# One PSUM bank for C, copied behind both exponentials of a unit, in the state space layer of a 12-layer decoder kernel

## The reference, cut to what matters

```python
dA = exp(delta[..., None] * A)                        # (b, t, 512 channels, 16 states)
dBu = delta[..., None] * Bm[:, :, None, :] * u[..., None]
def step(h, inp):
    dA_t, dBu_t, C_t = inp
    h = dA_t * h + dBu_t
    y = einsum('bdn,bn->bd', h, C_t)
    return (h, y)
...
delta = softplus(einsum('blr,dr->bld', dt, Wdt) + bdt)
```

## Time and profile before

| | |
|---|---|
| timed runs | 4219.53, 4219.45, 4218.51 us; median 4219.45 |
| span of the profiled execution | 4219.3 us (0.15 under the median; the profile gives no time of its own beside the span) |
| busy over the span | PE 89%, DVE 73%, ACT 54%, POOL 33% |
| scans L1255 | 512, 590.7 us |
| products L1260 | 176, 215.0 us |
| exponentials L1220 | 512, 345.7 us |
| copies of C L1233 | 176, 103.1 us |

### The profile page before, as it was taken

One profiled execution on the slowest core, in us unless ns is written; L12 is line 12 of the kernel. 1 busy time (PEld: TensorE's weight loads), 2 busy tenths in 40 slices (PEclk: granted clock), 3 DMA queues, 4 the chain that ended last, 5 costly groups with the idle time before them and its releaser, 6 DMA issues. The chain is left out here.

```text
span 4219.3 us, 57578 instructions
## 1 busy us (share of the span) xinstructions
PE 3754.1 (89%) x20106; PEld 2591.3 (61%) x20106; DVE 3071.9 (73%) x7148; ACT 2286.6 (54%) x5527; POOL 1378.4 (33%) x937
## 2 busy tenths in 40 slices
PE   5777878777999998999999999888899889889998
PEld 2323333223666667998788887555566558645777
DVE  6989899897666667666787886677577784554777
ACT  5676767754644442222455556757677652343446
POOL 3989899995000000000233223366321100010000
PEclk8989989898999999999999999889999999988999
DMA  3444434344000000000000001000000000100000
GB/s 117 142 132 146 148 125 156 130 152 146 1 1 1 1 1 33 21 31 1 14 1 1 1 1 42 2 14 1 12 2 2 19 23 1 42 1 20 1 1 21
DMA packets 83283, 180.17 MB, mean 43 GB/s; under 512 B 9035, under 2 KB 14259, under 8 KB 80307
## 3 DMA queue, kind: packets, MB, share of 16 engines
q1 hardware_dynamic: 82995, 176.49, 12.5%
HBM read 173.84 MB, written 2.62 MB: 42 GB/s over the span
## 5 line engine op out<-in xcount | busy, mean ns | idle before, releaser
L209 PE MATMUL PS<-db,cst 128*128 128x512 f32 x1024 | 537.2, 671 | 159.7 <-DVE db L1260 159.7
L1255 DVE TENSOR_TENSOR_SCAN db<-PS,db 128x512 f32<-128x512 f32 x512 | 590.7, 1204 | 36.7 <-ACT PS L1220 27.9
L209 PEld LDWEIGHTS PS<-db,cst 128*128 128x128 f32 x1024 | 205.2, 211 | 466.9 <-DVE db L1260 244.6
L216 PE MATMUL PS<-cst,p 128*128 128x128 f32 (+1 forms) x2880 | 393.3, 282 | 48.1 <-DVE pt L3295 16.7
L216 PEld LDWEIGHTS PS<-cst,p 128*128 128x128 f32 (+1 forms) x2880 | 332.9, 147 | 106.7 <-issue 35.9
L209 PE MATMUL PS<-xnT,W 128*128 128x256 f32 (+2 forms) x1072 | 330.7, 455 | 19.4 <-ACT pt L2826 7.9
L1201 POOL TENSOR_TENSOR db<-W,b 128x1024 f32<-128x1024 f32 x128 | 312.5, 2470 | 1.9 <-PE PS L209 1.8
L1201 POOL TENSOR_TENSOR db<-du,b 128x1024 f32<-128x1024 f32 x128 | 307.9, 2432 | 6.6 <-PE PS L209 5.8
L209 PEld LDWEIGHTS PS<-xnT,W 128*128 128x128 f32 (+1 forms) x1072 | 210.2, 200 | 137.9 <-issue 89.0
L2035 POOL TENSOR_TENSOR rb<-rb,tb 128x512 f32<-128x512 f32 x32 | 42.9, 1342 | 758.2 <-DVE tb L2030 758.2
L1693 ACT ACTIVATE p<-PS,sm 128x333 f32<-128x333 f32 x320 | 168.7, 538 | 164.8 <-DVE sm L1686 161.9
(11 more groups left out here) (469 smaller groups left out, 8512.2 us busy)
## 6 DMA issues: line engine op xcount, KB each, us to landing
b<-bc_rows SPq DMA_DIRECT2D x256, 256.0 KB, 3.4
c<-bc_rows SPq DMA_DIRECT2D x256, 256.0 KB, 3.5
W<-in_we SPq DMA_DIRECT2D x9, 1024.0 KB, 4.8
W<-in_w SPq DMA_DIRECT2D x1, 4224.0 KB, 12.3
W<-in_w SPq DMA_DIRECT2D x1, 4122.5 KB, 14.0
W<-in_w SPq DMA_DIRECT2D x1, 4100.0 KB, 12.3
W<-in_w SPq DMA_DIRECT2D x1, 2313.0 KB, 8.3
X<-in_x SPq DMA_DIRECT2D x4, 512.0 KB, 14.5
```

Source lines behind the costliest of these rows:

```text
L209: ins = T.matmul(out, l, r, start=first and i == 0, stop=last and i == len(pairs) - 1)
L216: ins = T.transpose(bank[0:m, c:c + r], s, ident[0:r, 0:r])
L1255: V.tensor_tensor_scan(db[:, f, r], self.ring.PS[:, self.BANKS[x % 3], r], db[:, f, r], 0.0, ALU.mult, ALU.add).then_inc(self.sc.sem, 1)
```

## The change

CBANKS becomes (4,): C always goes to bank 4, and bank 3 stays in the ring, which so has four banks in this layer, two for y and two that go round. The copy of C moves on ACT from between the two exponentials of its unit to behind both. With one bank it waits until the product of the vector unit before it is done, h(n), where before it waited for the one before that, h(n - 1).

```diff
-    CBANKS = (3, 4)
+    CBANKS = (4,)
...
             C.activation(bank[:, :, lo:hi], split(self.delta[d], 4)[:, 2 * p + f, :].rearrange(
                 "p (b s) -> p b s", b=2)[:, :, lo:hi], ACT.Exp,
                 scale=self.As[d][:, 2 * p + f, s:s + 1]).then_inc(self.aa.sem, 1)
-            if f == 0 and not self.on_pool(i):
-                self.act_c(e, i)
+        if not self.on_pool(i):
+            self.act_c(e, i)

     def cbank(self, i):
-        return self.ring.PS[:, self.CBANKS[(i - self.pools(i)) % 2], :]
+        return self.ring.PS[:, self.CBANKS[0], :]

     def act_c(self, e, i):

         e.wait_ge(*self.cd_of(i))
-        e.wait_ge(*self.h(i - self.pools(i) - 1))
+        e.wait_ge(*self.h(i - self.pools(i)))
         e.eng.activation(self.cbank(i), self.c_[i % 4], ACT.Copy).then_inc(self.ca.sem, 1)
```

## The result

The changed kernel takes 4232.3 us (median of 20 runs, 4212.17 to 4234.45); the kernel before, run beside it, 4219.57 us (20 runs). The ratio is 1.0022, 95% interval [1.0012, 1.0031]: about 9 us slower by the ratio, 5 to 13 by its interval, where 8.6 was forecast. The medians lie 12.7 us apart, since the times of the changed kernel fall into two groups (4 of the 20 at 4212 to 4215, 16 at 4229 to 4234) and the median takes no account of the small one. The profiled execution has a span of 4229.7 us.

The account below looks back on a forecast made before the run. DVE, busy 888.8 of the layer's 961 us, was taken to set the pace. Waits of 14.5 us less 5.6 for the ring's bank gave 8.9, taken as 8.6: about 4228 us (+0.2%), own range 4223 to 4233.

Parts of the forecast that it names:

- Gate SiLU: Four piles on ACT behind a second unit: each DVE wait becomes 2.95 us, 7.3 us lost in all.
- ABS of odd k: Delta chains of k = 3, 5, 7: fourth evacuation and ABS start 1.64 us later, 4.9 us lost in all.
- waits 1.6 us longer in sum: Sign of being right: DVE's waits for ACT in the k = 3, 5, 7 chains grow by 1.6 us in sum.
- Square root: The next layer's square root, unit 12 mod 16, starts 2.31 us later with SILU's pile behind it; 2.3 us lost.
- Ring bank: Delta chains of k = 1, 2, 4, 6: a second bank going round lets delta matmuls come earlier; 5.6 us gained.
- The start: Start of the layer, where PE waited for banks too: may give back some tenths of a us.
- Part 3: Second exponential comes 0.52 us earlier where ACT is late; DVE waited for the first, so nothing is gained.
- Wrong if the y waits move by more than 2 us: Sign of being wrong: DVE's waits for PE ahead of y move over 2 us in either direction.
- the ring's bank reaches nothing: Rival, chance 0.17: PE's low clock makes the delta matmul late, not the bank; only the 14.5 us remain, 4234.
- ACT's being held costs nothing: Rival, chance 0.10: long piles on ACT start as before, only the 5.6 us gain counts, 4214.
- the second exponential is waited for: Rival, chance 0.05: DVE waited for the second exponential, so 25 waits shrink by 0.52, 13.0 us; 4215.
- The copy in DVE's path: Rival, chance 0.05: copy falls into DVE's path in the steady run, 0.2 us for each of 96 units; 4247.

Follow-up runs that it names:

- held at the gates: Kernel before, with the copy behind both exponentials and the later wait only at the four units ahead of a gate SiLU; 4221.3 us, ratio 1.0020.
- the shortened pile: Kernel before, C's second bank lent to the ring at times, copy behind both exponentials, each gate's last evacuation one step earlier; 4215.8 us, ratio 0.9999.
- first pair of traces: First profiles of the kernel before and of the changed kernel; medians 4219.57 and 4232.3 us, ratio 1.0022.
- all piles moved: Changed kernel with gate SiLU one step later, delta chains of k = 3, 5, 7 and the first square root one step earlier; 4231.3 us, ratio 1.0038.
- second pair of traces: Kernel before and changed kernel, both unchanged, profiled a second time; 4218.3 us (ratio 1.0008) and 4232.6 us (ratio 1.0037).
- the kernel without it: Changed kernel with bank 3 left idle, so three banks in the ring as before; 4242.9 us, ratio 1.0058.
- held copies: Kernel before, copy moved and waiting later at chosen units only: without long piles (1.0000), at gate SiLUs (1.0020), at ABS and square root (1.0030).
- the order alone: Kernel before with only the copy moved behind both exponentials, two banks for C and the old wait; 4221.8 us, ratio 1.0014.

## Why the prediction was right

- **What bounds the kernel.** Right: DVE's path carried every term, and DVE waited for no copy.
- **Gate SiLU, 7.3 us.** Measured 7.4, all four waits 2.96 for a forecast of 2.95, alone again in the kernel held at the gates. The rule of the room behind a unit also gave the 0.5 of the shortened pile, but with 4.0 us of room for two banks and a copy behind both exponentials, worked out later; the 4.4 of the prediction would give 0.1.
- **ABS of odd k, 4.9 us.** DVE's L1144 starts 1.64 us later, the number forecast. But the 1.64 does not stay as it is: 1.1 of it is won back right behind (at k = 3 waits of 0.41 and 0.79 us become 0 and 0.22), and 1.7 is lost anew, since L1144 and L1157 themselves get longer beside POOL (3.13 for 2.02, 2.50 for 1.92). So 2.2 us a chain remain, 6.6 in all, and that the term is no further off is luck. The sign "waits 1.6 us longer in sum" did not come: they are 0.5 longer, and the rest stands in the length of DVE's own instructions.
- **Square root, 2.3 us.** 2.4.
- **Ring bank, k = 2, 4, 6 and k = 1, 5.6 us.** 5.9 by the first pair of traces, 7.5 by the second, in which the kernel before had the longer waits at k = 2 and 4. The Trainium skill, Perfetto Trace Analysis, Optimizing Tensor Performance, has groups rotate through different PSUM banks; the trace agrees, and more than I took from it. The bank also makes these chains deaf to PE's clock: 17 of the 18 waits at k = 2, 4, 6 in the six profiles with two banks to go round and the copy behind both exponentials are 1.76 or 1.77 at granted clocks from 0.50 to 1.00 (the other is 0.59, where all piles moved), against 2.96 to 5.04 at k = 2 with one bank. And it keeps the late copy from costing another 6.9 us at odd k.
- **The start, "some tenths".** 2.1 us in the first pair of traces, 1.7 of it PE's clock, and 0.8 in the second: L1144 starts at 53.92 and 52.77 before, at 51.83 and 51.98 now. The term was not one of order.
- **Part 3, order gains nothing.** No gain by it in the kernel before, as said. That it costs nothing is not shown there (mark 11 us later, time 1.0014), and with one bank for C it is worth 13 to 20 us, since it keeps the held copy out from between the exponentials.
- **"Wrong if the y waits move by more than 2 us."** They moved by 0.7 in all from the first trace of before to the first of the change, but by 4.8 from the second to the second (8.2 to 13.0), and by 2.6 between the two traces of the kernel before. So this sign did come in one pair, and it was the right thing to fear. The next layer's 2.8 us was in no term.
- **The sum, 8.6 us.** Without the start, the terms of the forecast add up to 10.5 in the first pair of traces and 8.9 in the second, where 8.9 was forecast: the mechanism is right. That the layer came to 7.7 is partly luck: the ABS term is 1.7 too small, and the start, by PE's clock, takes 1.8 more back than forecast. In the second pair of traces the layer is 12.9 longer.
- **The rivals.** That the ring's bank reaches nothing fell to the kernel without it. That ACT's being held costs nothing, and that the second exponential is waited for, fell to the kernels with held copies and with the order alone. The copy in DVE's path didn't occur, and no copy waits for its transfer with the change (before, 21 did, for 17.0 us in all). POOL took up no loss: from 60 to 1029 us it is busy for 877.3 us.

## What to carry to other kernels

A copy that waits for its one buffer costs nothing by itself and delays all that its engine has queued behind it (so it goes behind what the bound engine wants next); compute, for each long pile, the room up to the next instruction that the bound engine wants, and look only at piles longer than that. Two changes that each pay for the other (here a bank taken from one user and given to another) are to be measured apart as well as together, since neither has a price of its own: the ring's bank is worth 5.9 us at the places of the forecast, and 15.9, the start left out, when it is taken from the changed kernel. Where an engine's clock moves by stretches, read the waits that the order fixes, from two profiles, and not the end time of one.

## What the runs showed of the hardware

DVE's L1144 has two inputs in SBUF. It takes 1.23 us with POOL idle. In the kernel before, at k = 3, it starts at 343.63, inside the first of these two instructions of POOL, and ends at 345.65, 1.09 after that one's end:

```profile
342.21 2.35 POOL L1201 TENSOR_TENSOR db<-W,b 128x1024 f32<-128x1024 f32 x1
344.53 3.34 POOL L1201 TENSOR_TENSOR db<-W,b 128x1024 f32<-128x1024 f32 x1
```

The second took 1.0 us more. The rows read as if DVE went in at the boundary and POOL waited for it; that would be why a later start inside POOL's instruction made L1144 shorter, and an earlier one, in the change, longer. The Trainium skill, SBUF — State Buffer, Who interferes with whom, says that DVE and GpSimd contend for a shared pair of ports, that the pair is an exclusive lock, and that a DVE instruction with two SBUF inputs contends with a GpSimd instruction that reads SBUF. These rows agree. What it doesn't explain is the 12.90 us, in which DVE let five boundaries between POOL's instructions pass and came in only when POOL had nothing left; it happened at k = 3, 5 and 7 alike (12.90, 11.49, 12.74), and what decides between the first boundary and the sixth is open.
